# Staging the first loads in four transfers, one more round of filler waits on TensorE, and a first output block in halves, in a tiled three-einsum kernel

## What is computed

```python
Kf = jnp.einsum('bjd,ed->bje', F, K_w)
S = jnp.einsum('bid,bjd->bij', F, Kf)
out = jnp.einsum('bij,ijd->bid', S, W)
out = out + jnp.einsum('bid,ed->bie', F, Q_w)
```

## Time and profile before

| what | value |
|---|---|
| device time, three runs | median 608.06 us (607.44 to 609.15) |
| profiled execution, its own time | 608.0 us |
| span of its trace | 606.2 us |
| TensorE busy | 597.5 us, 99% |
| VectorE busy, ScalarE busy | 398.7 us, 401.5 us (66% each) |
| mean granted TensorE clock | 0.997 of full |

### The profile page before, as it was taken

How to read it: one execution, slowest core, us unless ns; L and a number is a source line. 1 busy time by engine, 2 the same in 40 slices (tenths; PEclk the granted TensorE clock), 3 DMA queues, 4 the chain that set the end, 5 groups by cost and what they waited for, 6 DMA issues and landing times.

```text
span 606.2 us, 17908 instructions
## 1 busy us (share of the span) xinstructions
PE 597.5 (99%) x7693; PEld 527.0 (87%) x7693; DVE 398.7 (66%) x412; ACT 401.5 (66%) x698; POOL 0.2 (0%) x4
## 2 busy tenths in 40 slices
PE   9999999999999999999999999999999999999995
PEld 7888989889898898988889898898988989889894
DVE  6556757567685665947659475686756768567376
ACT  7978393874938659295692947839387493865830
POOL 0000000000000000000000000000000000000000
PEclk9999999999999999999999999999999999999998
DMA  8543847548575575755647566385755757457177
GB/s 324 239 141 145 322 169 282 199 177 312 189 281 173 212 262 208 280 200 208 246 183 284 204 248 241 140 322 173 285 197 186 304 196 282 173 211 259 66 279 278
DMA packets 29452, 137.60 MB, mean 227 GB/s; under 512 B 3264, under 2 KB 4032, under 8 KB 21312
## 3 DMA queue, kind: packets, MB, share of 16 engines
q1 hardware_dynamic: 20592, 75.38, 31.5%
q10 hardware_dynamic: 8784, 61.08, 28.4%
HBM read 69.34 MB, written 67.11 MB: 225 GB/s over the span
## 4 chain that ended last, share of the span: by engine, by line
PE 98%; DVE 1%; issue 1%; DVEq 0%
PE ps L501 20%; PE ps L440 20%; PE ps L442 19%; PE ps L441 19%; PE ps L527 18%; DVE o_sb L371 1%; PE ps L557 1%; DVEq L46 0%; PE ps L457 0%; PE ps L461 0%; PE ps L459 0%; DVE o_sb L380 0%; DVE f_hi L385 0%
## 5 line engine op out<-in xcount | busy, mean ns | idle before, releaser
L336 DVE TENSOR_TENSOR f_lo<-f_ring,f_hi 128x1024 fp32r<-128x1024 f32 x124 | 151.8, 1224 | 169.6 <-ACT f_hi L214 167.9
L228 ACT ACTIVATE q_out<-ps 128x512 f32<-128x512 f32 x256 | 156.9, 613 | 6.4
L219 ACT ACTIVATE kf<-ps 128x512 f32<-128x512 f32 x256 | 155.9, 609 | 3.4
L371 DVE TENSOR_TENSOR o_sb<-ps,q_out 128x1024 f32<-128x1024 f32 x127 | 145.1, 1213 | 19.3 <-PE ps L527 19.3
L237 ACT ACTIVATE s_t<-ps 128x512 f32<-128x512 f32 x32 | 19.1, 598 | 176.5 <-PE ps L501 176.5
L501 PE MATMUL ps<-f_ring,kf 128*64 128x64 f32 x4096 | 124.1, 222 | 0.4 <-issue 0.4
L501 PEld LDWEIGHTS ps<-f_ring,kf 128*64 128x64 f32 x4096 | 121.6, 138 | 2.9 <-issue 0.8
L527 PEld LDWEIGHTS ps<-s_t,w_sb 64*128 64x128 f32 x2048 | 115.6, 188 | 5.6 <-issue 5.6
L527 PE MATMUL ps<-s_t,w_sb 64*128 64x128 f32 x2048 | 118.6, 274 | 0.0
L440 PE MATMUL ps<-f_hi,k_hi 128*128 128x512 f32 x254 | 100.7, 397 | 0.0
L440 PE MATMUL ps<-f_hi,q_hi 128*128 128x512 f32 x256 | 99.9, 390 | 0.0
(11 more groups left out here) (36 smaller groups left out, 164.3 us busy)
## 6 DMA issues: line engine op xcount, KB each, us to landing
out<-o_sb SPq DMA_DIRECT2D x127, 512.0 KB, 3.5
f_ring<-f_t ACTq DMA_DIRECT2D x58, 1024.0 KB, 4.8
f_ring<-f_t SPq DMA_DIRECT2D x4, 1024.0 KB, 10.4
w_sb<-w SPq DMA_DIRECT2D x1, 2048.0 KB, 18.8
f_ring<-f SPq DMA_DIRECT2D x6, 256.0 KB, 5.1
out<-o_sb SPq DMA_DIRECT2D x2, 256.0 KB, 2.4
f_ring<-f SPq DMA_DIRECT2D x3, 128.0 KB, 2.6
f_ring<-f ACTq DMA_DIRECT2D x1, 128.0 KB, 4.3
```

The source lines that it names most:

```text
L219: nc.scalar.activation(kf[:, c // 2, c % 2 * CK:(c % 2 + 1) * CK, :, :].rearrange("d k h i -> d (k h i)"), ps[:, 2 * c % 8, :], COPY).then ...
L228: nc.scalar.activation(q_out[:, t % 2, :, :].rearrange("d i (h b) -> d i h b", h=2)[:, :, :, at:at + CK], q_bank(t * CHUNKS + c).rearrange ...
L336: nc.vector.tensor_tensor(f_lo[:, v % SPLIT, :], f_unit(v), f_hi[:, v % SPLIT, :].bitcast(F32), ALU.subtract).then_inc(flo_done, 1)
L371: nc.vector.tensor_tensor(o_sb[:, n % OBUF, :, :], ps[:, bank:bank + 2, :], q_out[:, t % 2, :, :].rearrange("d (s m) b -> d s (m b)", s=2) ...
```

## The change

1. **First loads.** One new input, `first`, holds K^T, F's first 512 columns, Q^T and F's next 512 columns side by side. It is loaded in four transfers (two of 384 columns, two of 256) into output buffers that are not yet in use: two from SyncE, two from ScalarE. Before there were six (two of 128 columns, four of 256), three from each queue. VectorE now rounds the first 256 columns of F itself; chunk 1's K product is no longer in halves. Chunks 0 and 1 are loaded a second time, behind chunks 2 to 7, into their places in `f_ring`, for scores(0), which now waits for them.
2. **Filler waits.** FILL becomes 466 for tile 1 (round 0), 108 for tiles 2 to 14, and 128 for tile 15.
3. **Output layout.** In an output buffer the two halves of the rows now alternate by row, so `sum_out` reads and writes through one more dimension of its access patterns. The host's reordering follows.
4. **Last tile's first block.** It writes four banks, two rows into each pair; `o_half` tells VectorE when the first pair is done, and each `half_sum` adds one pair. The last tile's later blocks use other banks (`row_bank`).

```diff
-FILL = {2: 58}
-FILL.update((t, 108) for t in range(3, TILES - 1))
-FILL[TILES - 1] = 132
+FILL = {1: 466}
+FILL.update((t, 108) for t in range(2, TILES - 1))
+FILL[TILES - 1] = 128
...
+        raw = o_sb[:, 0:2, :, :, :].rearrange("d o x s b -> d (o x s b)")
+        k_raw, q_raw = raw[:, 0:D], raw[:, FC:FC + D]
+        f_raw = [raw[:, D:FC], raw[:, FC + D:2 * FC]]
...
+            return [0, 6, 4, 0, 2, 6, 4, 0][k] if t == TILES - 1 else 2 * k % 8
... SyncE
-            load_half(0)
-            load_half(1)
-            load_half(3)
+            sp.dma_start(raw[:, 0:CUT], first[:, 0:CUT]).then_inc(first_in[0], 16)
+            sp.dma_start(raw[:, FC + CUT:2 * FC], first[:, FC + CUT:2 * FC]).then_inc(first_in[3], 16)
             for c in range(2, PIECES):
                 load_first(c)
+
+            load_first(0)
+            load_first(1)
             for p in range(2, RING):
                 load_f(p)
... ScalarE
-            act.dma_start(k_raw, k_t).then_inc(k_in, 16)
-            act.dma_start(q_raw, q_t).then_inc(q_in, 16)
-            act.dma_start(f_half_cols(2), f_0[1, :, half_cols(0)]).then_inc(f_half[2], 16)
-            act.wait_ge(k_in, 16)
+            act.dma_start(raw[:, CUT:FC], first[:, CUT:FC]).then_inc(first_in[1], 16)
+            act.dma_start(raw[:, FC:FC + CUT], first[:, FC:FC + CUT]).then_inc(first_in[2], 16)
+            act.wait_ge(first_in[0], 16)
             nc.scalar.activation(k_hi[:, :], k_raw, COPY).then_inc(khi_done, 1)
-            split_half(0)
-            split_half(1)
-            act.wait_ge(q_in, 16)
+            act.wait_ge(first_in[1], 16)
+            nc.scalar.activation(f_hi[:, 0, half_cols(1)], f_raw[0][:, half_cols(1)], COPY).then_inc(fhi_first, 1)
+            act.wait_ge(first_in[2], 16)
             nc.scalar.activation(q_hi[:, :], q_raw, COPY).then_inc(qhi_done, 1)
-            split_half(2)
-            split_half(3)
+            act.wait_ge(first_in[3], 16)
+            nc.scalar.activation(f_hi[:, 0, piece_cols(1)], f_raw[1], COPY).then_inc(fhi_first, 1)
... VectorE
                 nc.vector.tensor_tensor(
-                    o_sb[:, n % OBUF, :, :], ps[:, bank:bank + 2, :],
-                    q_out[:, t % 2, :, :].rearrange("d (s m) b -> d s (m b)", s=2)[:, :, k * IR * P:(k + 1) * IR * P],
+                    o_sb[:, n % OBUF, :, :, :].rearrange("d x s b -> d s x b"),
+                    ps[:, bank:bank + 2, :].rearrange("d s (x b) -> d s x b", x=IR),
+                    q_out[:, t % 2, :, :].rearrange("d (s m) b -> d s m b", s=2)[:, :, k * IR:(k + 1) * IR, :],
                     ALU.add).then_inc(out_done, 1)
...
+            dve.wait_ge(first_in[0], 16)
+            nc.vector.tensor_copy(f_hi[:, 0, half_cols(0)], f_raw[0][:, half_cols(0)]).then_inc(fhi_dve, 1)
+            dve.wait_ge(fhi_dve, 1)
+            low_half(0)
             dve.wait_ge(khi_done, 1)
             nc.vector.tensor_tensor(k_lo[:, :], k_raw, k_hi[:, :].bitcast(F32),
                                     ALU.subtract).then_inc(klo_done, 1)
-            low_half(0)
+            dve.wait_ge(fhi_first, 1)
             low_half(1)
             dve.wait_ge(qhi_done, 1)
             nc.vector.tensor_tensor(q_lo[:, :], q_raw, q_hi[:, :].bitcast(F32),
                                     ALU.subtract).then_inc(qlo_done, 1)
-            low_half(2)
-            low_half(3)
+            low_first(1)
...
-            dve.wait_ge(o_done, n + 1)
+            dve.wait_ge(o_half, 1)
             dve.wait_ge(q_copied, TILES * CHUNKS)
             dve.wait_ge(o_stored[n % OBUF], n // OBUF * 16)
-            half_sum(0, 0).then_inc(out_half, 1)
-            half_sum(0, 1).then_inc(out_done, 1)
+            half_sum(0).then_inc(out_half, 1)
+            dve.wait_ge(o_done, n + 1)
+            half_sum(1).then_inc(out_done, 1)
... TensorE
-                    for x in range(FILL.get(t, 0) * c // CHUNKS, FILL.get(t, 0) * (c + 1) // CHUNKS):
-                        pe.wait_ge(zeros_done, 1)
+                    if t >= 1:
+                        for x in range(FILL[t] * c // CHUNKS, FILL[t] * (c + 1) // CHUNKS):
+                            pe.wait_ge(zeros_done, 1)
...
+                        if e == 0:
+                            for c in range(2):
+                                pe.wait_ge(f_first[c], 16)
...
+                    at, col = (bank + 2 * (x // 2), x % 2 * P) if split else (bank, x * P)
...
+                    if split and x == IR // 2 - 1:
+                        ins.then_inc(o_half, 1)
...
+                    if t == TILES - 1 and k >= 3:
+
+                        pe.wait_ge(out_half if k == 3 else out_done, 1 if k == 3 else t * UNITS + k - 3)
+                    elif k >= 4:
```

More of the change, by code:

```diff
@@ L26 @@
 FIRST = 4
+FC = D + BANK
+CUT = D + BANK // 2
 PIECES = FIRST * TOK // BANK
@@ L35, with build @@
 LATE = 2
-FILL = {2: 58}
-FILL.update((t, 108) for t in range(3, TILES - 1))
-FILL[TILES - 1] = 132
+FILL = {1: 466}
+FILL.update((t, 108) for t in range(2, TILES - 1))
+FILL[TILES - 1] = 128
 BOTH = [v for v in range(FIRST, TILES * UNITS) if v in (4, 5) or v >= UNITS and v % UNITS in (0, 4, 6)]
-def build(nc, f_0, f_t, k_t, q_t, w, out):
+def build(nc, first, f_0, f_t, w, out):
     with ExitStack() as ctx:
@@ L66, in build @@
         q_out = sbuf("q_out", [D, 2, N, P])
-        o_sb = sbuf("o_sb", [D, OBUF, 2, IR * P])
-        k_raw, q_raw = s_t[:, 0, :], s_t[:, 1, :]
+        o_sb = sbuf("o_sb", [D, OBUF, IR, 2, P])
+        raw = o_sb[:, 0:2, :, :, :].rearrange("d o x s b -> d (o x s b)")
+        k_raw, q_raw = raw[:, 0:D], raw[:, FC:FC + D]
+        f_raw = [raw[:, D:FC], raw[:, FC + D:2 * FC]]
         k_hi = sbuf("k_hi", [D, D], F32R)
@@ L80, in build @@
         ps = psum("ps", [P, 8, BANK])
-        f_half = [sem(f"f_half{n}") for n in range(4)]
+        first_in = [sem(f"first_in{n}") for n in range(4)]
         f_first = [sem(f"f_first{n}") for n in range(PIECES)]
         f_in = [sem(f"f_in{n}") for n in range(RING)]
-        k_in, q_in, w_in = sem("k_in"), sem("q_in"), sem("w_in")
+        w_in = sem("w_in")
         o_stored = [sem(f"o_stored{n}") for n in range(OBUF)]
@@ L95, in build, with row_bank @@
         s_done, s_copied, s_copied_act = sem("s_done"), sem("s_copied"), sem("s_copied_act")
-        o_done, out_done, out_half = sem("o_done"), sem("out_done"), sem("out_half")
+        o_done, out_done = sem("o_done"), sem("out_done")
+        o_half, out_half = sem("o_half"), sem("out_half")
+        def row_bank(t, k):
+            return [0, 6, 4, 0, 2, 6, 4, 0][k] if t == TILES - 1 else 2 * k % 8
         def q_bank(c):
@@ L185, in _ @@
             slot = t * UNITS % OBUF
+            half = o_sb[:, slot, :, :, :].rearrange("d (h x) s b -> d h (x s b)", h=2)
             sp.wait_ge(out_half, 1)
-            sp.dma_start(out[t, 0, :, 0:IR * P], o_sb[:, slot, 0, :]).then_inc(o_stored[slot], 16)
+            sp.dma_start(out[t, 0, :, 0:IR * P], half[:, 0, :]).then_inc(o_stored[slot], 16)
             sp.wait_ge(out_done, t * UNITS + 1)
-            sp.dma_start(out[t, 0, :, IR * P:2 * IR * P], o_sb[:, slot, 1, :]).then_inc(o_stored[slot], 16)
+            sp.dma_start(out[t, 0, :, IR * P:2 * IR * P], half[:, 1, :]).then_inc(o_stored[slot], 16)
             for k in range(1, UNITS):
@@ L309, in low_half @@
             def low_half(h):
-                dve.wait_ge(fhi_first, h + 1)
-                nc.vector.tensor_tensor(f_lo[:, 0, half_cols(h)], f_half_cols(h), f_hi[:, 0, half_cols(h)].bitcast(F32),
+                nc.vector.tensor_tensor(f_lo[:, 0, half_cols(h)], f_raw[0][:, half_cols(h)], f_hi[:, 0, half_cols(h)].bitcast(F32),
                                         ALU.subtract).then_inc(flo_first, 1)
@@ L315, in low_piece @@
                 slot, cols = c // 2 % SPLIT, piece_cols(c)
-                nc.vector.tensor_tensor(f_lo[:, slot, cols], f_cols(c), f_hi[:, slot, cols].bitcast(F32),
+                nc.vector.tensor_tensor(f_lo[:, slot, cols], f_raw[1] if c == 1 else f_cols(c), f_hi[:, slot, cols].bitcast(F32),
                                         ALU.subtract).then_inc(flo_first, 1)
             def low_first(c):
-                dve.wait_ge(fhi_first, (c + 7) // 2)
+                dve.wait_ge(fhi_first, (c + 3) // 2)
                 low_piece(c)
@@ L331, in both_first @@
                 nc.vector.tensor_copy(f_hi[:, c // 2 % SPLIT, piece_cols(c)], f_cols(c)).then_inc(fhi_dve, 1)
-                dve.wait_ge(fhi_dve, c // 2)
+                dve.wait_ge(fhi_dve, c // 2 + 1)
                 low_piece(c)
@@ L350, in both_f @@
                 nc.vector.tensor_copy(f_hi[:, v % SPLIT, :], f_unit(v)).then_inc(fhi_dve, 1)
-                dve.wait_ge(fhi_dve, 3 + sum(1 for x in BOTH if x <= v))
+                dve.wait_ge(fhi_dve, 4 + sum(1 for x in BOTH if x <= v))
                 low_unit(v)
@@ L450, in q_product, with k_halves @@
                       f_lo[:, c // 2 % SPLIT, piece_cols(c)]).then_inc(q_done, 1)
[L452 to L456, removed]
```

(32 more changed lines are left out.)

23 lines of the change are left out of this document (8 added, 15 removed).

## The result

The changed kernel takes 610.66 us (median of 6 runs, 610.46 to 610.79), the kernel before 608.15 (6 runs, 607.31 to 609.15). The ratio is 1.0041, 95% interval 1.0028 to 1.0054: slower by 0.4%. That is 1.1 us above the forecast of 609.6 and inside its range of 608.2 to 612.2. It is past 609.9, the mark of 0.3% that the forecast set for "slower"; "no change", which it held likeliest, is not what came.

The account below looks back on a forecast made before the run. TensorE, busy 597.5 of 606.2 us, was taken as the bound. From 608.0: opening -0.8, last tile -0.45, filler waits +3.8, stalls -1.7 and +0.8 gave 609.65, say 609.6 us; range 608.2 to 612.2.

Parts of the forecast that it names:

- Filler waits: Project(1), round 0: 242 filler instructions outrun the sequencer's lead, so rows(0) starts later; cost 3.8 us.
- 15 x 0.106 + 0.02 = 1.61 us: Project(1): sequencer time per chunk, 15 instructions plus 0.02 for six matmuls, against 1.36 to 1.38 us on the array.
- upper bound of 4.3: Project(1): cost in us if each of 242 filler instructions takes 0.11 us, with nothing for the matmuls.
- Rival C: Project(1): filler waits stay hidden and the gains at both ends remain, 605.9 us, faster; chance 0.12.
- Opening: First loads: chunk 1's data comes earlier, its six matmuls end at 7.5 instead of 8.27; gain 0.8 us.
- that product ends near 6.2: Opening: chunk 0's Q product, starting at 5.57 us, ends near 6.2, as chunk 0's chain hardly moves.
- rival B: Opening: the four loads bring nothing because the last lands at 5.8 us as before; 610.4 us, chance 0.08.
- Borders: Scores phases: borders move to 38 to 40 behind the first score; stalls total 0.8 us instead of 1.7.
- rival A: Scores: every phase stalls as the instruction request comes 0.1 us later among stores; 0.8 becomes 3.8, 612.6 us; chance 0.10.
- Last tile: End: the first part needs eight pairs instead of sixteen, so VectorE's sums start earlier; gain 0.45 us.
- Every sum and store follows 0.45 earlier: Last tile: VectorE starts near 592.4 us, and all later sums and stores move by the same 0.45 us.
- Sum: Whole kernel: 608.0 - 0.8 - 0.45 + 3.8 - 1.7 + 0.8 = 609.65, say 609.6 us.

Follow-up runs that it names:

- Experiments 9: Changed kernel without tile 1's 466 waits and with tile 2 at 58; first data in six transfers instead of four: 609.61 us, ratio 1.0033.
- 10: As experiment 4's neighbour above with six transfers, but Q^T alone releases its rounding and chunk 1's halves are awaited together: 608.65 us, ratio 1.0018.
- experiment 4: Kernel before with only the changed FILL (466, 108, 128); loads, layout and last tile as before: 611.93 us, ratio 1.0058.
- experiment 5: Changed kernel without tile 1's waits, tile 2's waits 6 instead of 58, borders 66 instead of 38 behind the first score: 615.50 us, ratio 1.0126.
- experiment 3: Changed kernel with 978 waits for tile 1 instead of 466, 256 filler instructions more: 638.32 us, ratio 1.0490.
- experiment 2: Changed kernel with tile 1's waits cut from 466 to 233 and tile 2's raised from 108 to 337: 607.22 us, ratio 0.9983.

## Why the prediction was right in its mechanism and short in its sum

**Filler waits** decided, as forecast, and the mechanism is shown from four sides: gone without them, hidden when spread, 27.8 us for 256 more, and the same 4.3 us in the kernel before. The size was off: I took 3.8 us and it is 4.25. Of the sum, it was the term "15 x 0.106 + 0.02 = 1.61 us" for a chunk that was small. The count, 242, and the 0.106 us inside a chunk were right. The 0.02 us for six matmuls was small: the wider gaps at the changes of chunk add 0.05 us at most of them and 0.17 at the widest (48.65 us), 1.1 us in all where the sum had 0.3. A chunk so takes 1.64 us; the chunk of 1.74, from 45.62 to 47.36, has 16 instructions instead of 15. The sum also has a slip of 0.1 the other way: 34.8 + 26.0 is 60.8 and not 60.9. The upper bound of 4.3 held. Rival C was wrong: what sets the pace of such waits is the 0.106 us and the gaps, not the 51 ns.

The Trainium skill, page "Runtime: NRT & Kernel Launch", section "Instruction fetch mechanics", gives an issue floor of about 20 cycles an instruction. The trace doesn't bear that floor out as the price of these waits: they start 0.106 us apart, twice the 51 ns that one lasts.

**Opening**: 0.8 forecast, 0.5 measured. The transfers landed at 4.6 us at the latest, close to the 4.3 that I took. The mis-sized step is "that product ends near 6.2": chunk 0's Q product started at 5.68, later than the 5.57 of before, as its K product waits for VectorE's rounding and both subtractions in a row, and ended at 6.4. Experiments 9 and 10 bear out that the third transfer is the late one: 4.2 and 4.3 us, then 3.5 and 5.7. But the opening isn't one number: the same loads landed up to 1.6 us later in the base's trace. Q^T comes in one transfer of 192 KB with half of chunk 1's data; it took 5.1 us there, 3.4 in the changed kernel's trace, and TensorE idled 1.11 us ahead of chunk 0's Q product. Chunk 2's K product starts at 7.6 to 8.2 us in eight of the nine traces with four transfers and at 9.4 in the base's; with the old loads it starts at 8.27 and, in experiment 4, at 9.01. So from execution to execution the opening differs by as much as the gain, and rival B's case occurs with four transfers too, in one trace of nine.

**Borders**: 1.7 to 0.8 forecast, 1.85 to 0.8 measured (with the stall behind tile 1's scores), but the size agrees by luck. I had let the 0.63 us of tile 15 go with the rest and spread 0.8 over 15 ordinary tiles; in the trace one ordinary tile lost 0.1 and tile 15 kept 0.65. That the break would move with the border was right (144 or 145 to 147 pairs, and 153, 161 and 179 in the experiments). That nothing in the place 38 ends the stalls was right too. What rival A named, stalls in every phase behind a later request, does come, but between 38 and 50 and not at 38. My later theory F, that the packet's start is fixed by the stores alone, fell with experiment 5.

**Last tile**: 0.45 forecast, 0.3 measured. The step that failed is "Every sum and store follows 0.45 earlier". The first half starts 0.42 us earlier, but the first sum of a whole block, at 2.10 us behind rows(15)'s start instead of 2.41, shows only 0.31 of it. The trace tells why: that sum waits for TensorE's second block. The block's last pair starts 1.78 us behind rows(15)'s start and the sum 0.32 behind that; in the kernel before, the first half sum followed the first block's last pair (0.89) by the same 0.32, to 1.21. So TensorE's pace, and no longer VectorE's, sets where the run of whole sums begins. The access patterns cost nothing: 1.214 us a sum against 1.213.

**Sum**: the three misses, 0.45 + 0.3 + 0.15 = 0.9, go one way and make most of the 1.1 us; another 0.15 is that I added to 608.0, where the kernel before has a median of 608.15 in six runs. My mark for "slower", 609.9, lay 0.3 us above my forecast, so misses that each stayed within their bounds were enough to pass it.

**The faster version** is the base of the experiments: opening, layout and last tile as changed, with 58 filler waits for tile 2 as before and none for tile 1. It stands at 0.9968 of the kernel before (0.9957 to 0.9979), where the changed kernel stands at 1.0041.

## What to carry to other kernels

Instructions that only wait are free as long as the engine's sequencer is ahead, and that is a budget per stretch: here 0.108 us each (experiment 3) against 1.36 us of array work in a chunk, so about twelve. Put padding where it is spread under that budget; a total that fits the kernel doesn't help if one round gets it all. And where a stall's place follows an instruction count, scan a few counts on both sides before keeping one: 34 and 38 mostly stalled a few tiles by 0.1 to 0.3 us, 50 and 66 all of them from tile 2 on, which made the kernel 1.6 to 1.7% slower than the base by the ratios.

## What the runs showed that I had not expected

The packet of the next block of instructions comes after its predecessor's border is reached, and it shares the DMA with the kernel's own stores. In tiles 2 to 14 it started 0.7 to 1.4 us behind the first score with one eighth of the stores, 1.3 to 2.1 with all of them at 34 and 38 (but for tile 2 of experiment 2, at 2.4), and 2.4 to 3.1 at 50 and 66.

Tile 15 took 8.27 to 8.33 us in eight of the nine traces with full stores and its border at 32 to 38, and its packet started at +2.3 to +2.4 there. The ninth is experiment 10's: the packet started at +1.73 and the phase took 7.72 us, as long as with narrow stores. So this stall goes with the late packet and not with the tile's place. Why the packet is late there so often stays open.

The granted clock rose at times between 4.6 and 6.9 us in 12 of the 13 traces, and at 10.6 in experiment 9's, where TensorE had idled 1.0 us before the rise. In the base's trace it had just risen, at 5.5, when TensorE idled 1.1 us, and it stayed up; in experiment 10's it had risen at 6.2, TensorE idled 1.8 us, and it fell at 9.6. In project(1) of experiment 3, where TensorE idled as much as it worked but in shorter pieces, it didn't fall.
